# A routed expert stage on one core: gate and up products with the weight stationary, and 71 tiles for 72

## The reference

```python
def reference(x, ctx_2048, ...):
    # (attention block, then the routed feed-forward block)
    x = x + _L0_xattn_ref(_layernorm(x), ctx_2048, ...)     # x: (8, 512, 512)
    x = x + _L0_ffn_ref(_layernorm(x), w_gate, wi_0, wi_1, wo)
    return x

def _L0_ffn_ref(x, w_gate, wi_0, wi_1, wo):                 # E, K, M = 8 experts, 2 of them a token, 256 wide
    xf = x.reshape(-1, 512)                                 # 4096 tokens
    top_logits, top_idx = jax.lax.top_k(jnp.dot(xf, w_gate), K)
    weights = jax.nn.softmax(top_logits, axis=-1)
    flat_idx = top_idx.reshape(-1)
    sort_order = jnp.argsort(flat_idx)
    sorted_x = jnp.take(xf, sort_order // K, axis=0)
    group_sizes = jnp.bincount(flat_idx, length=E)
    h0 = jax.lax.ragged_dot(sorted_x, wi_0, group_sizes)    # gate
    h1 = jax.lax.ragged_dot(sorted_x, wi_1, group_sizes)    # up
    inter = jax.nn.silu(h0) * h1
    out_sorted = jax.lax.ragged_dot(inter, wo, group_sizes)
    out = jnp.take(out_sorted, jnp.argsort(sort_order), axis=0).reshape(-1, K, 512)
    return jnp.einsum('tkd,tk->td', out, weights).reshape(b, s, d)
```

## Time and profile before

| | before |
|---|---|
| median of 3 runs | 2205.02 us (2200.27 to 2205.75) |
| the profiled execution's own time | 2211.22 us |
| its span, first to last instruction | 2209.5 us |
| mean granted TensorE clock | 0.939 |
| PE busy | 1849.1 us (84%) |
| PEld busy | 1264.9 us (57%) |
| DVE busy | 1795.7 us (81%) |
| ACT busy | 1351.7 us (61%) |
| POOL busy | 969.0 us (44%) |

### The profile page before, as it was taken

The page is one execution under the profiler, slowest core; times in us unless marked ns, Lnnn a source line. Parts: engine busy times, 40 slices in busy tenths (PEclk is TensorE's granted clock), DMA queues, the critical chain, the costliest instruction groups (busy, mean ns, idle before and its releaser), DMA issues. The chain is left out here.

```text
span 2209.5 us, 60580 instructions
## 1 busy us (share of the span) xinstructions
PE 1849.1 (84%) x24745; PEld 1264.9 (57%) x24804; DVE 1795.7 (81%) x2402; ACT 1351.7 (61%) x1944; POOL 969.0 (44%) x900
## 2 busy tenths in 40 slices
PE   1379998999988989998989898989986147999996
PEld 1247676666666666666666666667763012555553
DVE  4469999899998998998999999988996582666665
ACT  0347877777777777777777787777766431233222
POOL 0011653383265336434723553373435101677675
PEclk9889999999999999999999999999998556999998
DMA  2322332233233223323322331331221351566785
GB/s 86 99 80 56 96 93 53 78 103 85 59 99 101 61 74 100 95 56 87 108 79 62 105 105 44 88 108 56 65 54 49 99 159 62 176 200 218 242 264 176
DMA packets 152822, 225.40 MB, mean 102 GB/s; under 512 B 33860, under 2 KB 87108, under 8 KB 152544
## 3 DMA queue, kind: packets, MB, share of 16 engines
q1 hardware_dynamic: 130736, 166.89, 26.2%
q0 software_dynamic: 21808, 54.58, 8.0%
HBM read 131.37 MB, written 71.32 MB: 92 GB/s over the span
## 5 line engine op out<-in xcount | busy, mean ns | idle before, releaser
L764 DVE TENSOR_TENSOR a_p_low<-a_p 128x1024 f16<-128x1024 f32 (+1 forms) x896 | 1095.5, 1245 | 141.5 <-ACT a_p L642 133.6
L642 ACT ACTIVATE a_p<-ps_s 128x1024 f32<-128x1024 f32 (+1 forms) x896 | 862.6, 967 | 390.4 <-PE ps_s L493 382.1
L493 PE MATMUL ps_s<-a_q_stack,a_k_stack 96*128 96x512 f16 (+1 forms) x1664 | 516.0, 385 | 81.1 <-DMA a_k_stack<-a_k_parts 55.0
L604 PE MATMUL ps_o<-a_v,a_p 128*128 128x65 f16 (+1 forms) x6656 | 448.3, 195 | 19.3 <-ACT a_o_sums L668 8.9
L604 PE MATMUL ps_o<-a_v,a_p_low 128*128 128x65 f16 (+1 forms) x6656 | 448.0, 194 | 0.0
L526 PEld LDWEIGHTS ps_p<-wkv,a_ctx 128*128 128x128 f16 x4992 | 329.6, 99 | 166.1 <-DVE a_v L779 59.0
L526 PE MATMUL ps_p<-wkv,a_ctx 128*128 128x128 f16 x4992 | 378.7, 221 | 44.4 <-DVE a_v L779 44.1
L604 PEld LDWEIGHTS ps_o<-a_v,a_p 128*128 128x128 bf16 (+1 forms) x6656 | 352.7, 99 | 101.2 <-DVE a_p_low L764 26.9
L510 PE MATMUL ps_p<-a_ctx,wkv 128*128 128x384 f16 (+2 forms) x1536 | 347.6, 336 | 36.9 <-DVE a_ctx L402 34.2
L604 PEld LDWEIGHTS ps_o<-a_v,a_p_low 128*128 128x128 f16 (+1 forms) x6656 | 318.4, 98 | 0.0
L510 PEld LDWEIGHTS ps_p<-a_ctx,wkv 128*128 128x128 f16 x1536 | 147.7, 98 | 184.6 <-DVE a_ctx L402 30.9
(11 more groups left out here) (232 smaller groups left out, 2211.9 us busy)
## 6 DMA issues: line engine op xcount, KB each, us to landing
a_k_stack<-a_k_parts SPq DMA_DIRECT2D x384, 80.0 KB, 2.1
d_ys<-f_y SPq DMA_DIRECT2D x72, 256.0 KB
a_ctx_raw<-in_ctx_dram SPq DMA_DIRECT2D x64, 192.0 KB, 2.5
a_q_stack<-d_q_t SPq DMA_DIRECT2D x96, 128.0 KB, 3.6
a_xm<-in_x_dram SPq DMA_DIRECT2D x8, 1024.0 KB, 5.9
a_ctx_raw<-in_ctx_dram SPq DMA_DIRECT2D x32, 256.0 KB, 4.6
d_q_t<-a_q_parts SPq DMA_DIRECT2D x32, 256.0 KB, 2.7
d_q_full<-a_xm SPq DMA_DIRECT2D x32, 256.0 KB, 2.9
```

The costliest lines, as they stand in the source:

```text
L493: mm = pe.matmul(t["ps_s"][s % 2][0:r, n * N:(n + 1) * N], t["k_stack"][v % 2][0:TERMS * DH, j, kt * P:kt * P + r], t["q_stack"][v % 2][0: ...
L604: mm = pe.matmul(t["ps_o"][:, q * VC:(q + 1) * VC], part[0:r, n * N + q * P:n * N + (q + 1) * P], val, start=(g == 0 and n == 0 and low == ...
L642: act.activation(t["p"][s % NP][0:r, 0:len(tiles) * N], t["ps_s"][s % 2][0:r, 0:len(tiles) * N], ACT.Exp, scale=float(DH) ** -0.5 / WSCALE ...
L764: dve.tensor_tensor(t["p_low"][s % NP][0:r, 0:n], full, high, ALU.subtract).then_inc(lows, 1)
```

## The change

`hide` makes the product with its operands exchanged: for each of four blocks `f` of 128 of the 512 gate and up columns, the block of `wi` is the stationary operand and the turned tokens are the moving one, 128 columns. So gate and up come out with their columns on partitions and the tokens along the free axis, and `parts` has already the form that `produce` needs as its stationary operand. `turn_inner` and `copy_inner` go away with their buffers, `produce` follows its tile one step earlier, and `TILES` is 71. The diff, cut to its core:

```diff
-TILES = 72
-assert TILES * P >= B * N * TOPK + E * (P - 1)
+TILES = (B * N * TOPK + E * (P - 1)) // P
+assert B * N * TOPK % P == 0
...
             for n in range(NY):
-                sp.wait_ge(y_out[n], 16 * (TILES // NY))
+                sp.wait_ge(y_out[n], 16 * len(range(n, TILES, NY)))
...
-                for m in range(TERMS * CC):
-                    c, term = m // TERMS, m % TERMS
-                    x_part, w_part = (0, 1, 0)[term], (0, 0, 1)[term]
-                    last = pe.matmul(ps_h[n % 2][:, :], xt[n % 2][:, x_part, c, :],
-                                     t["wi"][:, bass.ds(e, 1), w_part, c, :].rearrange("p a f -> p (a f)"),
-                                     start=(m == 0), stop=(m == TERMS * CC - 1))
+                for f in range(2 * MB):
+                    for m in range(TERMS * CC):
+                        c, term = m // TERMS, m % TERMS
+                        x_part, w_part = (0, 1, 0)[term], (0, 0, 1)[term]
+                        last = pe.matmul(ps_h[n % 2][:, f * P:(f + 1) * P],
+                                         t["wi"][:, bass.ds(e, 1), w_part, c, f * P:(f + 1) * P]
+                                         .rearrange("p a f -> p (a f)"),
+                                         xt[n % 2][:, x_part, c, :], start=(m == 0), stop=(m == TERMS * CC - 1))
                 last.then_inc(hidden, 1)
 
-            def turn_inner(n):
-                pe.wait_ge(split, n + 1)
-                if n >= 2:
-                    pe.wait_ge(i_copied, n - 1)
-                for part in range(2):
-                    for m in range(MB):
-                        at = (part * MB + m) * P
-                        last = pe.transpose(ps_i[n % 2][:, at:at + P], parts[n % 2][:, part, m * P:(m + 1) * P],
-                                            k["id16"][:, :])
-                last.then_inc(i_turned, 1)
-
             def produce(n, e):
-                pe.wait_ge(i_copied, n + 1)
+                pe.wait_ge(split, n + 1)
...
-                    last = pe.matmul(ps_y[n % 2][:, :], it[n % 2][:, i_part, c, :],
+                    last = pe.matmul(ps_y[n % 2][:, :], parts[n % 2][:, i_part, c * P:(c + 1) * P],
...
-            for n in range(TILES + 2):
+            for n in range(TILES + 1):
                 if n < TILES:
                     experts[n] = pe.value_load(t["expert_of"][0:1, n:n + 1], min_val=0, max_val=E - 1)
                     hide(n, experts[n])
-                if 1 <= n <= TILES:
-                    turn_inner(n - 1)
                 if n + 1 < TILES:
                     turn_x(n + 1)
-                if n >= 2:
-                    produce(n - 2, experts[n - 2])
+                if n >= 1:
+                    produce(n - 1, experts[n - 1])
...
                 act.wait_ge(multiplied, n + 1)
+                if n >= 2:
+                    act.wait_ge(produced, n - 1)
                 act.copy(parts[n % 2][:, 0, :], inner[n % 2][:, :]).then_inc(high, 1)
-                if n >= 2:
-                    finish(n - 2)
-            finish(TILES - 2)
+                if n >= 1:
+                    finish(n - 1)
             finish(TILES - 1)
...
-            def copy_inner(n):
-                dve.wait_ge(i_turned, n + 1)
-                if n >= 2:
-                    dve.wait_ge(produced, n - 1)
-                dve.tensor_copy(it[n % 2][:, :, :, :].rearrange("p s m n -> p (s m n)"),
-                                ps_i[n % 2][:, 0:2 * MB * P]).then_inc(i_copied, 1)
...
-                if 1 <= n <= TILES:
-                    copy_inner(n - 1)
```

More of the change, by code:

```diff
@@ L1653, in run_experts @@
         parts = [sb(f"parts{n}", [P, 2, FF], F16) for n in range(2)]
-        it = [sb(f"it{n}", [P, 2, MB, P], F16) for n in range(2)]
         y = [sb(f"y{n}", [P, C], F32) for n in range(NY)]
@@ L1659, in run_experts @@
         ps_h = banks(nc, held, ["f_ph0", "f_ph1"])
-        ps_i = banks(nc, held, ["f_pi0", "f_pi1"], F16)
         ps_y = banks(nc, held, ["f_py0", "f_py1"])
@@ L1666, in run_experts @@
         cleared, begun, added = sem("f_cleared"), sem("f_begun"), sem("f_added")
-        x_turned, x_copied, hidden, gated, multiplied, high, split, i_turned, i_copied, produced, y_ready = (
+        x_turned, x_copied, hidden, gated, multiplied, high, split, produced, y_ready = (
             sem("f_" + n) for n in ("x_turned", "x_copied", "hidden", "gated", "multiplied", "high", "split",
-                                    "i_turned", "i_copied", "produced", "y_ready"))
+                                    "produced", "y_ready"))
         @block.gpsimd
@@ L1731, in hide, with produce @@
                     pe.wait_ge(multiplied, n - 1)
-                for m in range(TERMS * CC):
-                    c, term = m // TERMS, m % TERMS
-                    x_part, w_part = (0, 1, 0)[term], (0, 0, 1)[term]
-                    last = pe.matmul(ps_h[n % 2][:, :], xt[n % 2][:, x_part, c, :],
-                                     t["wi"][:, bass.ds(e, 1), w_part, c, :].rearrange("p a f -> p (a f)"),
-                                     start=(m == 0), stop=(m == TERMS * CC - 1))
+                for f in range(2 * MB):
[6 more added lines that the diff above has]
+                                         xt[n % 2][:, x_part, c, :], start=(m == 0), stop=(m == TERMS * CC - 1))
                 last.then_inc(hidden, 1)
-            def turn_inner(n):
+            def produce(n, e):
                 pe.wait_ge(split, n + 1)
-                if n >= 2:
-                    pe.wait_ge(i_copied, n - 1)
-                for part in range(2):
-                    for m in range(MB):
-                        at = (part * MB + m) * P
-                        last = pe.transpose(ps_i[n % 2][:, at:at + P], parts[n % 2][:, part, m * P:(m + 1) * P],
-                                            k["id16"][:, :])
-                last.then_inc(i_turned, 1)
-            def produce(n, e):
-                pe.wait_ge(i_copied, n + 1)
                 if n >= 2:
```

## The result

The kernel after takes 2291.12 us (median; 2288.26 to 2299.94), the kernel before 2205.39 in the same comparison: a ratio of 1.0367, interval 1.0334 to 1.0399. It is slower, as forecast, and by more: 86 us by the medians for a forecast of 63, inside the range by one microsecond. The profiled execution took 2290.43 us, 79.2 more than that of before.

What follows compares the result with a forecast made beforehand. The full TensorE array bounded the kernel at 4.555 us a tile; after the change its sequencer would, at 5.55. Tiles +64.6, last `hide` +1.1, end -2.1, `route` -0.5 make +63 on 2205: 2268 us, range 2250 to 2292.

Steps and rivals of the forecast that it cites:

- What bounds the kernel now: Expert stage before the change: TensorE's array is full at 4.555 us a tile; register instructions 0.125 us apart lie hidden under matmuls.
- (2): TensorE's sequencer in the new `hide`: 32 register instructions for 8, 0.125 us apart plus one late gap, 3.9 us.
- (3): Tile length is the longer of two loops, through the sequencer 5.5 us, through the data 5.57; taken 5.55, bounds 5.40 to 5.70.
- B: Rival: in `hide`, loads and short matmuls are slower than transposes, up to 6.9 us a tile, some 2361 us; chance 0.05.
- the data loop: Tile's path through `hide`, the transposes of `turn_x` and the copy back to the sequencer: 5.57 us, 1.67 beside the 31 gaps.
- (4): Work under the tile's loop, `produce`'s matmuls, DVE, ACT, POOL, SP, gathers and ACT's new wait: costs 0.
- (5): Whole-kernel sum: tiles +64.6 us, last `hide` +1.1, end -2.1, first tile 0, `route` -0.5; together +63.
- A: Rival: the sequencer is not the limit in `hide`, the array's 4.44 us a tile holds, 2190 us; chance 0.08.
- C: Rival: TensorE's clock falls as `hide` pauses; 8.6 us a tile, 2480 us, or 2340 for a quarter of the time; chance 0.05.
- D: Rival: no change in the kernel's time, needing a register-instruction pace of about 0.09 us by accident; chance 0.02.

## Why the forecast was right, and where its size was off

**What bounds the kernel now: right.** Loads and short matmuls start 0.056 us apart, and the array is full before. The run without register instructions in `hide` shows the array's own time, 4.422 us a tile for the forecast 4.44.

**The sequencer's pace, (2): right, with a term too small.** The plain gap is the one read from the earlier trace rows. What I had as "one late gap" a tile is one in eight register instructions, about four in `hide`. So `hide` takes 4.10 us and not 3.9, on the average gap 0.132. The eight register instructions of the kernel before have one late gap a tile, and I carried over one a tile where the rows had one in eight: the earlier trace rows gave 0.13, and I multiplied by 0.125.

**The two loops, (3): the term that was mis-sized.** 5.55 was forecast, with bounds of 5.40 and 5.70, and 5.777 measured, outside them: 69 x 0.23 = 16 us, all of the 79 - 63 by which the profiled times missed. That the median of 2291 still lies in the range is luck: my bounds from (3) ended at 2278 and with the coarse steps at 2285, and the last 7 us had been added for B, which is not what happened. Of the 0.23, 0.20 are the late gaps in `hide`. The rest of the loop was 1.67 in the forecast's sum through the data and 1.67 as measured, from the last register instruction of one `hide` to the first of the next. It is the sequencer's own path: the run with `turn_x` moved forward rules the data loop out as what sets it.

**What lies under it, (4): right.** DVE, ACT and POOL have more idle time than before, and nothing waits for the new wait of ACT.

**Once each, (5): right to a microsecond or two.** Last `hide` +1.4 for +1.1; the end -2.8 for -2.1; the first tile the same 5.30 us at the lower clock; in `route` the 64 matmuls are 46.7 us busy for 47.3, 0.6 less for the 0.5 taken, though the stage begins 0.4 later, with everything ahead of it in that:

```profile
L1488 PE MATMUL r_ps<-r_marks,r_lane_hot 128*128 128x426 f16 x64 | 46.7, 907 | 39.4 <-DVE r_marks L1605 39.4
```

One tile less is worth 3 us, and not 5, by a ratio that allows both.

**The rivals.** A, that the sequencer isn't the limit, fails on the kernel after and on the tile lengths of the table. Its price was about right: the runs with 16 and with no register instructions came to 2202 and 2195 us for its 2190, or to 0.9948 and 0.99 of the kernel before in the same comparison for its 0.993. B fails, as shown. C: the clock was 1.00 in the stretches of the stage shown, between 1900 and 2250 us, also with 48 register instructions and 396 matmuls in 50 us. Its price for a quarter of the time was summed wrong: a quarter of 69 x 3.05 is 53 us, which gives some 2320 and not 2340. D is met by another number of register instructions, and 24 of them came near it with 1.0039. The break-even is (4.555 - 1.67) / 0.132 + 1 = 23 register instructions, against the 32 of the change. My other form of it, a pace of 0.093 at 32, was not tried.

The Trainium skill's 81 ns a matmul for a sustained stream of loads and 128-column matmuls ("TensorE: Matmul & The Clock Gate", section "Back-to-back issue gap") comes out right for the kernel after, 0.080 by the arithmetic above, and would have given about 2288 us. The trace without register instructions disagrees with it: 0.056. So the figure was met here for another reason, and taken as the array's pace it would have said that the change can't be mended.

What stays open: what the late gap is. It came with 16, 24, 32 and 48 register instructions a tile, in one gap of eight whatever the number of matmuls between (by the start times from 1900 to 2100 us); no run was made for its cause. Whether a program that works out the addresses anew only where the expert changes would come near the run with none (0.99 of the kernel before) was not tried either.

## What to carry to other kernels

Where an operand's address is known at run time only, count the blocks that get an address, not just the columns: each costs TensorE's sequencer 0.132 us here, whatever the length of the matmuls behind it, so an address for each 1.5 matmuls needs matmuls longer than 0.088 us, and 128 columns (0.056) are not enough where 512 (0.215) are. PE's busy time doesn't show such a limit, because short matmuls are recorded longer than they hold the array: compare counts in equal stretches, the idle time of the loads, and the start times of the register instructions. Before work is cut into smaller pieces, ask for the sequencer's loop through one tile as one asks for the array's, and for what holds the sequencer back at its start.

## What the runs showed of the hardware

A register instruction costs TensorE's sequencer 0.124 us, and one in eight some 0.066 more, while loads and matmuls with fixed addresses pass at next to nothing: 9 pairs between two sequencer instructions 0.2 us apart. Three pairs behind one register instruction go at the array's pace (4.458 us a tile with 16 of them, for 4.422 with none). A read of a value from memory with its assert costs the sequencer 0.65 us, and was free when 0.8 us of waiting lay over it (0.9997) and not when it came four times over (1.0525). The sequencer doesn't run ahead of the array without bound: with 17 pairs handed on and not begun, its next instructions went at the array's pace, in the kernel before and in the one with four more reads alike.
